# Layer norm's small arithmetic moved from VectorE to GpSimd, in a fused attention and mixture-of-experts block

## What is computed

```python
x = x + tanh(g_xattn) * attention(layernorm(x), ctx, ctx)     # 32 query heads, 8 kv heads, D = 32
x = x + tanh(g_ffn) * moe(layernorm(x))                       # 64 choices, top 8, 32 of them real experts

def layernorm(x, eps=1e-5):
    m = mean(x, -1); v = var(x, -1)
    return (x - m) / sqrt(v + eps)
```

## Time and profile before

| | us |
|---|---|
| median of three runs | 2283.83 |
| lowest and highest | 2280.14, 2286.11 |
| the profiled execution | 2268.57 |
| its span, on which all times below stand | 2266.8 |
| PE busy in the span | 2090.5 (92%) |
| DVE busy | 1472.1 (65%) |
| ACT busy | 1246.2 (55%) |
| POOL busy | 1096.5 (48%) |

### The profile page before, as it was taken

How to read it: one execution, slowest core, us unless ns; L and a number is a source line. 1 busy time by engine, 2 the same in 40 slices (tenths; PEclk the granted TensorE clock), 3 DMA queues, 4 the chain that set the end, 5 groups by cost and what they waited for, 6 DMA issues and landing times.

```text
span 2266.8 us, 48610 instructions
## 1 busy us (share of the span) xinstructions
PE 2090.5 (92%) x14776; PEld 1226.8 (54%) x14777; DVE 1472.1 (65%) x2463; ACT 1246.2 (55%) x1833; POOL 1096.5 (48%) x1241
## 2 busy tenths in 40 slices
PE   5999998988999787899999999999999999999996
PEld 2555454544545444456556564744656776454464
DVE  6789889998989674346446582833564875463384
ACT  3787767766776536235445463633554764353364
POOL 3127878887887766224323351622353653240262
PEclk8999999999999998999999999999999999999998
DMA  5478566665664854657666593955694986664582
GB/s 149 128 197 178 158 171 178 157 177 149 175 161 115 258 151 129 201 158 212 181 181 194 169 294 90 295 176 148 172 260 140 293 243 179 185 196 149 148 249 52
DMA packets 569277, 407.81 MB, mean 180 GB/s; under 512 B 213558, under 2 KB 489142, under 8 KB 569200
## 3 DMA queue, kind: packets, MB, share of 16 engines
q1 hardware_dynamic: 506112, 334.10, 50.6%
q0 software_dynamic: 46336, 72.10, 13.4%
q10 hardware_dynamic: 16752, 0.65, 0.5%
HBM read 319.33 MB, written 103.16 MB: 186 GB/s over the span
## 4 chain that ended last, share of the span: by engine, by line
PE 49%; DVE 5%; issue 4%; ACT 2%; POOL 1%; DMA 0%; DVEq 0%; ACTq 0%; POOLq 0%
PE psum L1674 32%; PE psum L1704 15%; DVE xgt L1329 2%; PE psum L1614 2%; DVE wgu L1317 1%; DVE wdn L1322 1%; ACT wgu L941 0%; DVE a L1339 0%; DMA xg<-pairs,gslots 0%; ACT ys L970 0%; POOL lists L725 0%; ACT apair L962 0%; POOL spare L808 0%; ACT wdn L949 0%; POOL out_dram L828 0%
## 5 line engine op out<-in xcount | busy, mean ns | idle before, releaser
L1674 PE MATMUL psum<-xgt,wgu 128*128 128x224 f16 (+3 forms) x6336 | 877.9, 296 | 38.4 <-issue 20.5
L1674 PEld LDWEIGHTS psum<-xgt,wgu 128*128 (+1 forms) x6336 | 568.8, 98 | 346.7 <-issue 49.8
L808 POOL TENSOR_TENSOR spare<-spare 128x1 f32<-128x1 f32 x164 | 127.3, 776 | 814.6 <-PE psum L1704 424.2
L1704 PE MATMUL psum<-wdn,apair 128*128 128x512 f16 x1968 | 456.8, 382 | 21.9 <-issue 14.1
L1160 DVE TENSOR_REDUCE mx<-psum 128x2 f32<-128x512 f32 x512 | 327.2, 683 | 65.8 <-PE psum L1533 63.0
L1317 DVE SCALAR_TENSOR_TENSOR wgu<-wraw,wgu 128x1024 f16<-128x1024 f32 x264 | 318.2, 1215 | 30.5 <-ACT wgu L941 30.5
L725 POOL DMA_INDIRECT lists<-entry,dest x256 | 273.7, 1069 | 102.9 <-issue 68.8
L1329 DVE COPY xgt<-psum 128x1024 f16<-128x1024 f16 x256 | 166.9, 681 | 226.8 <-PE psum L1614 219.5
L1704 PEld LDWEIGHTS psum<-wdn,apair 128*128 128x128 f16 x1968 | 186.8, 98 | 226.9 <-issue 32.8
L1339 DVE SCALAR_TENSOR_TENSOR a<-psum,sg 128x512 f32<-128x512 f32 x132 | 90.8, 688 | 330.4 <-PE psum L1674 330.4
L924 ACT ACTIVATE prob<-psum 128x512 f32<-128x512 f32 x512 | 275.6, 593 | 48.3 <-PE psum L1546 46.9
(11 more groups left out here) (157 smaller groups left out, 1976.6 us busy)
## 6 DMA issues: line engine op xcount, KB each, us to landing
wraw<-in_L_ffn_w_gate_up_dram SPq DMA_DIRECT2D x264, 512.0 KB
wraw<-in_L_ffn_w_down_dram SPq DMA_DIRECT2D x132, 512.0 KB, 5.8
x<-in_x_dram SPq DMA_DIRECT2D x16, 1024.0 KB
xr<-in_x_dram SPq DMA_DIRECT2D x16, 1024.0 KB
out_dram<-x SPq DMA_DIRECT2D x16, 1024.0 KB
pairs<-xs SPq DMA_DIRECT2D x16, 1024.0 KB, 5.5
qs<-qh SPq DMA_DIRECT2D x248, 64.0 KB
qs<-ql SPq DMA_DIRECT2D x128, 64.0 KB
```

The lines of the kernel that those rows point to most:

```text
L1674: mm = pe.matmul(ps_gu[:, s, h, 0:UP_COLUMNS[nt]], w[:, a, k, :], xgt[:, c, k, 0:UP_COLUMNS[nt]], start=(k == 0 and (a, c) == (0, 0)), sto ...
L1704: mm = pe.matmul(psum[:, Y_BANK[i] + n2, :], apair[:, o, k, c * P:(c + 1) * P], w[:, a, k, :], start=(k == 0 and (a, o) == (0, 0)), stop=( ...
```

## The change

`veps` and `nmr` are no longer computed on VectorE. `power`, on GpSimd, now waits for the two aggregations (`var_ready`, counted twice a norm), computes the scaled variance, the power, the negated mean (a new tile `shift`) and their product, with a semaphore wait between each two, and releases `nmr_ready`. `rstd_ready` is gone. VectorE's `norm_var` only aggregates; before it overwrites `mv` it waits until the previous norm of the same kind has been finished on GpSimd. `norm_shift` is gone, and VectorE's count of its own instructions falls from 7 to 5 a norm. In slot 0 GpSimd now takes `norm1` and `max_pairs` first and both parts of `picks` after them.

```diff
+        shift = sb("shift", [P, 2, T2])
-        rstd_ready = sem("rstd_ready")
             def power(which, n):
 
-                pool.wait_ge(var_ready, n)
-                pool.tensor_tensor(rstd[:, which], veps[:, which], half[:], ALU.pow).then_inc(rstd_ready, 1)
+                scale = XS_SCALE ** -2
+                pool.wait_ge(var_ready, T2 * n)
+                chain(pool.tensor_scalar(veps[:, which], mv[:, which, :, 1], scale, LN_EPS * scale, ALU.mult, ALU.add))
+                chain(pool.tensor_tensor(rstd[:, which], veps[:, which], half[:], ALU.pow))
+                chain(pool.tensor_scalar(shift[:, which], mv[:, which, :, 0], -1.0, None, ALU.mult))
+                pool.tensor_tensor(nmr[:, which], shift[:, which], rstd[:, which], ALU.mult).then_inc(nmr_ready, 1)
...
                 for kv in range(KV):
-                    if kv == 0 and on(b, -3) and not early(b):
-                        picks(b - 3, 0)
                     if kv == 0 and on(b, 2):
                         norm1(b + 2)
                     if kv == 0 and on(b, 0):
                         max_pairs(b, 1)
                     if kv == 0 and on(b, -3) and not early(b):
+                        picks(b - 3, 0)
                         picks(b - 3, 1)
...
-            def norm_var(which, tally):
+            def norm_var(which, last_read, tally):
+                if last_read is not None:
+                    dve.wait_ge(nmr_ready, last_read)
                 tally.wait()
                 carry_wait(tally)
                 for t in range(T2):
-                    tally.add(dve.bn_aggr(mv[:, which, t], stats[:, which, t]))
-                tally.wait()
-                scale = XS_SCALE ** -2
-                dve.tensor_scalar(veps[:, which], mv[:, which, :, 1], scale, LN_EPS * scale, ALU.mult, ALU.add).then_inc(var_ready, 1)
-
-            def norm_shift(which, n):
-                dve.wait_ge(rstd_ready, n)
-                dve.scalar_tensor_tensor(out=nmr[:, which], in0=mv[:, which, :, 0], scalar=-1.0, in1=rstd[:, which],
-                                         op0=ALU.mult, op1=ALU.mult).then_inc(nmr_ready, 1)
+                    dve.bn_aggr(mv[:, which, t], stats[:, which, t]).then_inc(var_ready, 1)
...
-            N_A, N_OUT, N_R1, N_R2, N_W, N_R3 = 7, 1, 7, 26, 9, 8
+            N_A, N_OUT, N_R1, N_R2, N_W, N_R3 = 5, 1, 5, 26, 9, 8
...
-                        norm_var(1, tally)
+                        norm_var(1, None if is_first(b - 1) else nth_norm2(b - 2), tally)
...
-                        norm_var(0, tally)
-                    if kv == 1 and on(b, 2):
-                        norm_shift(0, nth_norm1(b + 2))
+                        norm_var(0, None if is_first(b + 2) else nth_norm1(b + 1), tally)
...
-                    if kv == 4 and on(b, -1):
-                        norm_shift(1, nth_norm2(b - 1))
```

## The result

The changed kernel takes 2331.09 us (median of four runs, 2327.37 to 2333.33), the kernel before, measured beside it, 2284.92: a ratio of 1.0207, 95% interval 1.0192 to 1.0221. The forecast was 2301, and its range ended at 2320. The direction was right and the size was not: +46 us against +17.

The account below looks back on a forecast made before the run. GpSimd's chain of work and fixed pauses, steps of 47.28 us, was taken as the bound. The terms -1.5 + 18.9 - 2.4 + 2 + 0 = +17 us on 2283.8 gave 2301 us, range 2286 to 2320.

Parts of the forecast that it names:

- closed chain: GpSimd's whole step: work, a fixed pause ahead of a scatter, work, setting TensorE's pace at the transpose; steps of 47.28 us.
- Item 1: Removing `veps`, `nmr` and the aggregation wait from VectorE: -1.5 us for four early steps, nothing in steps bound by GpSimd.
- Item 2: Scaled variance, shift and product added to GpSimd with semaphore waits: 0.86 us a norm, 22 norms, +18.9 us.
- Item 3: GpSimd's waits for ScalarE, mainly two for qf, go because GpSimd comes later: -2.4 us.
- Item 4: Picks moved behind norm and maxima pairs on GpSimd: no work added, possible wait for the aggregates, 0 to +12, taken +2 us.
- The margin of 0.3 us: At the first norm, VectorE's aggregates are ready (458.54) just before GpSimd asks for them (458.86).
- Item 5: ScalarE and VectorE newly waiting on GpSimd's norm: the transpose stays the last to wait, so 0 us.
- GpSimd waits for the aggregates in every step: Rival: the margin at the first norm turns negative, +12 to +38 us, 2312 to 2322, centre 2316; chance 0.13.
- VectorE's stall is the bound: Rival: the stall at `veps` sets the step, so removing `veps` and `nmr` saves 37 us, 2247 us; chance 0.11.
- The additions are covered by fewer meetings: Rival: long GpSimd meetings with VectorE instructions mostly fall into pauses, nearly paying for the additions; about 2284 us; chance 0.14.
- Steps of 48.7 to 49.2 us: Sign: distance between first maxima pairs grows from 47.28 us to this; steps under 47 us would be wrong.
- TensorE's wait for the pair: Sign: TensorE's pause at the transpose of GpSimd's second maxima pair grows from 0.42 us to between 1.5 and 5.

Follow-up runs that it names:

- old_order: The changed kernel, but with the first pick products ahead of the norm again, as in the kernel before: 2304.08 us, ratio 1.0087.
- before_again: The kernel before, unchanged, profiled a second time for a second trace: 2288.92 us.
- order_only: The kernel before with only the new order on GpSimd (picks after norm and maxima pairs), the norm's arithmetic still on VectorE: 2304.23 us, ratio 1.0084.

## Why the prediction was wrong, point by point

**The bound.** "GpSimd is therefore a closed chain" was read from the absence of waits. It was half of the truth. GpSimd does set TensorE's pace at the transpose in the changed kernel (pause 5.06 us) and in old_order (0.7 to 5.1); in the kernel before, TensorE was never far ahead of it (pauses of 0.40 to 0.42 us in the first execution, 0.11 at most in the second). But the loop goes from the transpose through TensorE and VectorE to the aggregates and back to GpSimd, and in leg A that way is nearly as long as GpSimd's own (in before_again: aggregates 19.6 us after the pair, GpSimd's question for them at 21.0 with the picks and mostly at 17.5 or 18.6 without).

**Item 1**, -1.5 us for the four early steps: the last three of them took 1.8 us less, but began 1.7 us later, so that of the 1.5 us about 0.1 was there at 179 us. **Item 2**, 0.86 us a norm, +18.9: measured 0.94 a norm. **Item 3**, -2.4 for the qf waits, can't be told apart from item 2. Items 1 to 3 together were +15 and old_order measured +20, so this half of the sum was right within 5 us. The estimate that the prediction worked out from the Trainium skill (GPSIMD Engine Reference, Key points), 1.26 us a norm, is too high here: 0.94 measured.

**Item 4**, +2 us, is the term that failed. After the additions' 20 us there remain 26 of the 46; the order alone, in order_only, cost 20. Its arithmetic asked what a missed margin costs, and left out the 2.6 us of the picks, with the reason that nothing was added by the new order. For a closed chain that is right. For two legs it isn't: the picks went from leg A, where the wait for the aggregates would have filled their place, to leg B, where nothing covers them. Leg B took +2.9 us for it (30.8 against 27.9), leg A gave back only 0.2 (20.4 against 20.6). The margin of 0.3 us was also the wrong number to lean on: the first execution had it in every step, but the second had -1.0 and -2.2 in its place, counted at the fourth `ql`, and in the changed kernel the aggregates come 20.3 us after the pair instead of 18.1.

**Item 5**, ScalarE's wait for the shift, 0: the wait appeared as foretold (32.6 us in nine), and TensorE still waited last at the transpose. Right.

**The rivals.** "GpSimd waits for the aggregates in every step" is what happened, and the prediction named its mark: long waits for the aggregates, "then item 4 was the cost". Its chance was 0.13 and its price too low, 2312 to 2322, because it too counted the wait and not the picks behind it. "VectorE's stall is the bound" is refuted as it was priced: old_order takes `veps` and `nmr` from VectorE and is slower. "The additions are covered by fewer meetings" fell as well: the meeting with VectorE's residual only changed its victim, `picked` at 489.05 (2.17 us) for the copy at 470.05.

**The marks.** Steps of 48.7 to 49.2 us were foretold; they are 51.2, and old_order's 48.4. TensorE's wait for the pair was to be 1.5 to 5 us; it is 5.06 in this step. The wait for the maxima was to fall from 2.16 below 1; its longest is 0.7.

## What to carry to other kernels

Where two engines work in a ring, cut the step at the points where one hands over to the other and add up the legs; a move of work between two legs is a change of time even when no instruction is added, and slack in one leg doesn't pay for work in the other. Before you put an instruction behind a wait, ask what will cover that wait once the instruction has left its place, and take the arrival of the other engine from several steps of more than one execution. The absence of a wait shows that an engine has no slack, but not that it alone is the bound: see by how much it could be relieved before another engine is the later one.

## What the runs showed of the hardware

**One VectorE instruction holds GpSimd up, whatever it meets.** VectorE's residual (two operands from SBUF, 2.35 us) lengthens one GpSimd instruction a step in every version. In before_again it is an indirect DMA, 2.69 us instead of 0.97; in the changed kernel the 32-element sum, 2.17 instead of 0.25:

```profile
464.87 2.35 DVE L1176 SCALAR_TENSOR_TENSOR x<-at,tg_at,xr 128x2048 f32<-128x2048 f32 x1 [0.22 <-DVE at L1167]
...
465.38 2.69 POOL L725 DMA_INDIRECT lists<-entry,dest  x1 [0.31 <-issue]
```

```profile
488.71 2.40 DVE L1173 SCALAR_TENSOR_TENSOR x<-at,tg_at,xr 128x2048 f32<-128x2048 f32 x1 [0.22 <-DVE at L1164]
```

The smaller `low_x` (1.22 us) does it too: in before_again it starts at 444.11 and `wpair`, 0.20 us elsewhere, takes 1.29 at 444.10. In both cases the GpSimd instruction ends at most 0.9 us behind VectorE's (468.07 and 467.22, 445.39 and 445.33). The Trainium skill (SBUF — State Buffer, Who interferes with whom) says that the later of the two is blocked until the first has finished. The first case agrees, with the DMA 0.5 us later; in the second the two starts lie 0.01 us apart, too close to tell which was first. The long `veps` of the kernel before agrees with the turns but not clearly with their order: it is recorded as starting at 458.58, ahead of the pick (458.86) behind which it ends.

**The price of a scatter.** An indirect DMA of one index per partition costs GpSimd 0.97 us and 0.30 of pause ahead of it, 1.27 in a row. Moving four of them moved 5.1 us.

**The same kernel on the same kind of chip.** The kernel before takes 2284 us on two of the chips that were used and 2265 on a third (13 runs, 2262.7 to 2268.74). Between its two profiled executions the 20 us lie in the passage to the expert part alone. Their cause is open, and ratios here are taken against runs on the same chip only.
